# The gated linear attention stage of a decoder layer, its eight groups rewritten

## The reference

```python
q = jax.nn.silu(x @ Wq); v = x @ Wv
log_f = jax.nn.log_sigmoid(x @ Wk + delta); k = -jnp.expm1(log_f)
# per head, over the tokens t:
S = S * jnp.exp(g_t)[..., None] + k_t[..., None] * v_t[..., None, :]
o_t = jnp.einsum('bhk,bhkv->bhv', q_t, S)
# then
o = o * jax.nn.sigmoid(x @ G1 @ G2)
og = og * jax.lax.rsqrt(jnp.mean(og * og, axis=-1, keepdims=True) + EPS)
x = layernorm(x + (og.reshape(B, T, E) * norm_w) @ Wo)
```

## Time and profile before

| | us |
|---|---|
| median of 3 runs | 784.97 (783.91 to 785.06) |
| span of the profiled execution | 781.0 |
| TensorE, VectorE, ScalarE, POOL busy in it | 583.7, 576.7, 404.8, 348.8 |
| first stage, start to the last write of X | 0 to 219.2 |

### The profile page before, as it was taken

One profiled execution on the slowest core, in us unless ns is written; L12 is line 12 of the kernel. 1 busy time (PEld: TensorE's weight loads), 2 busy tenths in 40 slices (PEclk: granted clock), 3 DMA queues, 4 the chain that ended last, 5 costly groups with the idle time before them and its releaser, 6 DMA issues.

```text
span 781.0 us, 18314 instructions
## 1 busy us (share of the span) xinstructions
PE 583.7 (75%) x4172; PEld 468.7 (60%) x4172; DVE 576.7 (74%) x1999; ACT 404.8 (52%) x1107; POOL 348.8 (45%) x445
## 2 busy tenths in 40 slices
PE   4576888778657899999999988239999999993000
PEld 1355666666546677777777756128888888883000
DVE  4888898898535788888988975676666666652998
ACT  1456654556224666666666653027666666663111
POOL 2611111011001137667667775637777777775000
PEclk9687787667656999999999985559999999998555
DMA  5000001000073012122121111243333333333653
GB/s 176 0 15 14 15 13 31 4 0 0 1 215 88 15 35 62 57 60 60 55 60 53 41 49 51 73 99 81 96 97 101 98 101 97 93 100 82 219 193 99
DMA packets 62705, 54.64 MB, mean 70 GB/s; under 512 B 16748, under 2 KB 52146, under 8 KB 62416
## 3 DMA queue, kind: packets, MB, share of 16 engines
q1 hardware_dynamic: 52816, 36.86, 17.1%
q0 software_dynamic: 8704, 16.87, 6.9%
q10 hardware_dynamic: 1152, 0.53, 0.3%
HBM read 29.96 MB, written 21.11 MB: 65 GB/s over the span
## 4 chain that ended last, share of the span: by engine, by line
PE 48%; DVE 19%; DMA 11%; issue 11%; SPq 4%; ACT 3%; POOL 2%; DVEq 1%; POOLq 0%; ACTq 0%
PE bank L781 6%; DMA ys<-yout,xin 5%; PE bank L788 4%; DMA xin<-xs 4%; PE bank L655 4%; PE bank L664 4%; PE bank L629 3%; PE bank L620 3%; DVE r L1450 3%; PE bank L646 3%; PE bank L539 3%; PE bank L773 2%; DVE Rq L1101 2%; DVE mx L1251 2%; PE bank L556 2%
## 5 line engine op out<-in xcount | busy, mean ns | idle before, releaser
L498 POOL DMA_INDIRECT ys<-yout,xin x144 | 145.8, 1013 | 54.4 <-issue 38.2
L479 POOL DMA_INDIRECT xs<-xrow,slots x128 | 130.5, 1019 | 50.7 <-issue 43.5
L996 ACT ACTIVATE hid<-bank,wcur 128x128 f32<-128x128 f32 x292 | 91.4, 364 | 41.1 <-PE bank L781 40.3
L781 PE MATMUL bank<-xinT,wcur 128*128 128x128 f32 x584 | 100.3, 295 | 0.6 <-issue 0.2
L1406 DVE COPY wcur<-wall 128x642 f32 x148 | 74.9, 508 | 20.9 <-DVE gates L1397 0.9
L788 PE MATMUL bank<-wcur,hid 128*128 128x128 f32 x576 | 88.5, 277 | 0.0
L1251 DVE TENSOR_REDUCE mx<-bank 128x4 f16<-128x308 f32 x128 | 60.0, 469 | 33.5 <-PE bank L629 31.9
L781 PEld LDWEIGHTS bank<-xinT,wcur 128*128 128x128 f32 x584 | 77.8, 194 | 8.5 <-issue 3.2
L1413 DVE TENSOR_TENSOR yout<-bank,wcur 128x128 f32<-128x128 f32 x144 | 42.0, 291 | 53.3 <-PE bank L788 51.9
L931 ACT ACTIVATE Ex<-bank 77x512 f32<-77x512 f32 x128 | 75.2, 588 | 5.1 <-PE bank L646 4.4
L788 PEld LDWEIGHTS bank<-wcur,hid 128*128 128x128 f32 x576 | 76.7, 194 | 0.0
(11 more groups left out here) (212 smaller groups left out, 1355.2 us busy)
## 6 DMA issues: line engine op xcount, KB each, us to landing
xin<-xs SPq DMA_DIRECT2D x156, 64.5 KB, 1.8
yin<-ys SPq DMA_DIRECT2D x16, 512.0 KB, 3.7
ys<-yout,xin POOLq DMA_INDIRECT x144, 2.3
xTg<-xT_dram SPq DMA_DIRECT2D x8, 256.0 KB, 2.8
X<-x_dram SPq DMA_DIRECT2D x1, 2048.0 KB, 8.3
x1s<-X SPq DMA_DIRECT2D x32, 64.0 KB
wall<-w_dram SPq DMA_DIRECT2D x1, 2048.0 KB, 8.5
X<-xrow SPq DMA_DIRECT2D x32, 64.0 KB
```

What stands on the lines that cost most here:

```text
L479: pool.indirect_dma_start(words, bass.IndirectOffsetOnAxis(ap=slots[p][:, r:r + 1], axis=0), xrow[p][:, r, 0:RW], None).then_inc(s(f"scatt ...
L498: pool.indirect_dma_start(ys, bass.IndirectOffsetOnAxis(ap=xin[p][:, :].bitcast(U32)[:, E:RW], axis=0), yout[p][:, :], None, bounds_check= ...
L781: mm = pe.matmul(psH[p % 3][:, c * P:(c + 1) * P], wcur[p % QUAD][:, c * P:(c + 1) * P], xinT[p % 4][:, :], start=True, stop=True)
L996: act.activation(hid[p % 3][:, c, :], psH[p % 3][:, c * P:(c + 1) * P], ACT.Gelu, bias=wcur[p % QUAD][:, 2 * I + c:2 * I + c + 1]).then_in ...
```

## The change

The changed stage computes the same sums with other tiles:

- Exponentials are taken of the raw projections in PSUM and capped afterwards; one logarithm and one exponential over 1536 columns serve forgetting, query and gate. The gate weight G1 G2 is multiplied out once.
- Distances to the anchors are formed for the middle token of each block of 8 (64 columns a level in place of 512). Level sides are the leaf sides times such small weights. Key sides, distances and `k` move to POOL; query sides stay on VectorE.
- Levels 64 and 32 are multiplied head by head, 64 rows each, into halves of one bank per head, and copied by ScalarE without a mask. Levels 16 and 8 keep masked copies. Leaves use 64-row tiles and one masked copy of 1024 columns.
- `attended` puts values on the stationary side, so its output is already turned; the head's mean square comes from a matmul with ones.
- Groups are written out, in a new order, and the DMAs of weights are split by first use.

```diff
-            sp.dma_start(xTg[0][:, :], A["xT"][:, 0:GC]).then_inc(s("xT_in0"), 16)
-            for name, t in zip(weights_dma, (wk, wq, wv, wo, g1, g2, delta, norm_w, cwq, cwqT, cwkvT, cwcT, rw, rb)):
+            sp.dma_start(wk[:, :], A["wk"]).then_inc(s("wk_in"), 16)
+            sp.dma_start(xTg[0][:, :], A["xT"][:, 0:GC]).then_inc(s("xT_in0"), 16)
...
@@ POOL, a group
+            def first_part_step(g):
+                keys1(g)             # k = ee * sg, 512 columns
+                leaf_keys(g)         # Kleaf = k * eK, 512; free(A_ps, 4 * g)
+                level_keys(g, 0)     # Lk = Kleaf * wK, 256 columns each
+                level_keys(g, 1).then_inc(s("keys_ready"), 1)
+                level_keys(g, 2).then_inc(s("keys_ready"), 1)
+                level_keys(g, 3).then_inc(s("keys_ready"), 1)
+                if g + 1 < NG:
+                    leaf_decay(g + 1)    # 512 columns
+                    level_decay(g + 1)   # 4 x 64 columns
@@ TensorE
+                for b in range(GB):      # near_levels: level 64, then level 32
                     for h in range(H):
+                        pe.matmul(psN[h][0:64, b * 64:(b + 1) * 64], Lk[0][HP[h], b * T:b * T + 64], Rq[0][HP[h], b * 64:(b + 1) * 64], start=True, stop=True)
+                for n in range(2):
+                    rows = slice(64 * n, 64 * n + 32)
+                    for b in range(GB):
+                        for h in range(H):
+                            mm = pe.matmul(psN[h][rows, 256 + b * 32:256 + (b + 1) * 32], Lk[1][HP[h], b * T + 64 * n:b * T + 64 * n + 32],
+                                           Rq[1][HP[h], b * 64 + 32 * n:b * 64 + 32 * n + 32], start=True, stop=True)
...
+                        mm = pe.matmul(psN[h][:, c], Kleaf[HP[h], c], Qleaf[HP[h], c], start=True, stop=True)   # leaves
...
+                        mm = pe.matmul(psO[HP[h], b * T:(b + 1) * T], v[g % 2][:, b * E + h * DH:b * E + (h + 1) * DH], AT[g % 2][:, h, b, :], start=True, stop=True)   # attended
...
+                pe.matmul(psM[:, :], headsum[:, :], osq[:, :], start=True, stop=True).then_inc(s("ms_ps"), 1)
...
+                    far_level(g - 1, 3)
+                    far_level(g - 1, 2)
+                    leaves(g - 1)
+                    forgets(g + 1)
+                    attended(g - 1)      # waits: taken, v_ready, near_taken
+                    queries1(g + 1)      # two matmuls of 512 columns
+                    head_sums(g - 1)
+                    values1(g + 1)
+                    near_levels(g)       # waits: keys_ready, query_sides, taken
+                    project_out(g - 1)
@@ ScalarE
+                act.activation(ee[:, 1:3, :], ps[:, 1:3, :], ACT.Exp, scale=-1.0).then_inc(s("exps"), 1)
+                act.activation(ll[:, :, :], ee[:, :, :], ACT.Ln, bias=1.0).then_inc(s("logs_ready"), 1)
+                act.activation(sg[g % 2][:, :, :], ll[:, :, :], ACT.Exp, scale=-1.0).then_inc(s("sig_ready"), 1)
...
+                    squares(g - 1)
+                    forget_exp(g + 1)
+                    query_exp(g + 1)
+                    head_scales(g - 1)   # ln and exp, 512 columns each
+                    logs(g + 1)
+                    near_take(g)
+                    sigmoids(g + 1)
+                    value_copy(g + 1)
+                    leaf_exp(g + 1)      # 2 x 512
+                    scales(g - 1)
+                    level_exp(g + 1)     # 2 x 256
+                    normal(g - 1)
@@ VectorE
+                    gated(g - 1)
+                    leaf_queries(g)
+                    level_queries(g, 2).then_inc(s("query_sides"), 1)   # 2 x (64 x 256)
+                    level_queries(g, 0)                                 # 128 x 256
+                    level_queries(g, 1).then_inc(s("query_sides"), 1)   # 128 x 256
+                    cap_forget(g + 1)    # 512 columns
+                    cap_query(g + 1)     # 1024 columns
+                    level_queries(g, 3).then_inc(s("query_sides"), 1)   # 2 x (64 x 256)
+                    head_norm(g - 1)
+                    scan(g + 1)
+                    residual(g - 1)
+                    level_take(g, 3)
+                    moments(g - 1)
+                    level_take(g, 2)
+                    combined(g - 1)
+                    leaf_take(g)         # 1024 columns
+                    shift(g - 1)
+                    query(g + 1)
```

More of the change, by code:

```diff
@@ L395, in _ @@
             setup_steps["masks"] = n
[L397 to L402, removed]
             def leaf_decay(g):
-                pool.wait_ge(s("scan_steps"), 2 * g + 1)
+                pool.wait_ge(s("scanned"), g + 1)
+                free(pool, "decay_exp", 2 * g - 1)
@@ L445, in _ @@
             setup_steps["cross"] = n
-            with pool.Fori(1, NG) as g:
-                key_logs(g)
-                leaf_decay(g)
+            for g in range(3, NG):
+                first_part_step(g)
             words = xs.rearrange("n w -> (n w)").unsqueeze(1)
@@ L503, in _ @@
         def _(pe):
[L504 to L513, removed]
[L514 to L522 removed]
+            psU, psQ, psG, psV = banks[0], banks[1], banks[2], banks[0]
@@ new lines, in _, with forgets, queries1 @@
+            psN, psL = banks[3:5], {2: banks[5], 3: banks[6]}
+            psO, psM, psY, psW = banks[7], banks[7], banks[7], banks[7]
+            HP = [slice(h * DH, (h + 1) * DH) for h in range(H)]
+            def forgets(g):
+                pe.wait_ge(s(f"xT_in{g % 2}"), 16 * (g // 2) + 16)
+                free(pe, "v_ready", g)
+                pe.matmul(psU[:, :], wk[:, :], xTg[g % 2][:, :], start=True, stop=True).then_inc(s("u_ps"), 1)
+            def queries1(g):
+                free(pe, "q_ready", g)
+                pe.matmul(psQ[:, :], wq[:, :], xTg[g % 2][:, :], start=True, stop=True)
+                pe.matmul(psG[:, :], wg[:, :], xTg[g % 2][:, :], start=True, stop=True).then_inc(s("qg_ps"), 1)
@@ L544, in leaves @@
[L544 to L552 removed]
+                pe.wait_ge(s("keys_ready"), 4 * g + 1)
@@ L565, in project_out @@
-            def project_out(g):
-                pe.wait_ge(s("oT_ready"), g + 1)
-                for b in range(GB):
-                    mm = pe.matmul(psY[:, b * E:(b + 1) * E], oT[:, b * T:(b + 1) * T], won[:, :], start=True, stop=True)
-                mm.then_inc(s("y_ps"), 1)
-            pe.wait_ge(s("weights_in"), WN)
-            pe.wait_ge(s("pool_setup"), setup_steps["masks"])
-            pe.wait_ge(s("won_ready"), 1)
-            project_in(0, 0, 16, first=True)
-            gates(0)
@@ L870, in step @@
+            act.wait_ge(s("ndelta_ready"), 1)
+            forget_exp(0)
+            act.wait_ge(s("wg_ps"), 1)
+            act.activation(wg[:, :], psW[:, 0:E], ACT.Copy).then_inc(s("wg_ready"), 1)
+            query_exp(0)
+            logs(0)
+            sigmoids(0)
+            value_copy(0)
+            leaf_exp(0)
+            level_exp(0)
+            act.wait_ge(s("dve_setup"), dve_setup["zeros"])
+            for g in range(NG + 1):
+                if g >= 1:
                     squares(g - 1)
-                if attend:
-                    decay(g, NL)
@@ L1123, in gated @@
[L1123 to L1130 removed]
+            psQ, psL, psO, psY = banks[1], {2: banks[5], 3: banks[6]}, banks[7], banks[7]
```

586 lines of the change are left out of this document (282 added, 304 removed).

## The result

The changed kernel takes 713.73 us (median of 4 runs, 711.67 to 715.5) against 784.5 us (783.91 to 785.06): ratio 0.9098, 95% interval 0.908 to 0.9116. The forecast was 703, its range 692 to 728.

The account below looks back on a forecast made before the run. VectorE bounds the first stage before the change, TensorE's queue after; that stage ends at 22.2 + 7 x 13.5 + 20.3 = 137.0 instead of 219.2 us, so span 698.8, plus 3.97 gives 703 us; range 692 to 728.

Parts of the forecast that it names:

- Start: First stage up to the first near-level matmuls: they begin at 22.2 us, after scan, POOL's distances and keys.
- Period: Time per group in the first stage: 11.3 / 0.90 + 0.9 = 13.5 us, taken seven times.
- TensorE's queue itself ends last: Walk through one group: TensorE's queue sets the period, with 0.5 us for the leaf copy and 0.4 for hand-overs.
- a sign that the walk missed a wait: Listed sign of error: TensorE waiting over 2 us a group for VectorE or ScalarE.
- the shared port sets the period: Rival: POOL's SBUF work blocks VectorE for half of its 7.2 us, 14.9 us a group, 713 us; chance 0.14.
- Tiles: TensorE's half-array matmuls run side by side: leaves and attended 0.97 us each, near levels 2.0 us a group.
- in series: Rival: half-array matmuls run one after the other, or drain; 18.8 us a group, 744 us; chance 0.11.
- Clock: TensorE's granted clock in the first stage, taken as 0.90, between 0.84 and the cross-attention stage's 1.00.
- end: Tail of the first stage, from the last near levels to its end: 20.3 us.
- Engine sums: Work per group after the change: VectorE 11.3 us, ScalarE 11.9, POOL 7.2, TensorE 11.3 at full clock.
- What follows: Stages behind the first: same code, started by the same transfer, so costed at nothing.
- 3.97: Microseconds by which the median of the runs stood above the profiled span, added to the 698.8 us span.

Follow-up runs that it names:

- e2: Changed kernel plus an unneeded 512-column GpSimd product, reading SBUF, behind the keys of seven groups; 0.9311 of the kernel before, unchanged control 0.926.
- e3: Changed kernel plus an unneeded 1400-column GpSimd memset, reading no SBUF, behind the keys of seven groups; 0.9316 of the kernel before, unchanged control 0.926.
- e9: Changed kernel with GpSimd's later-stage constants built early, plus the far level of half blocks of 8 moved ahead of the output projection; 0.9001 of the kernel before.
- e1: Changed kernel with GpSimd's constants for later stages built ahead of group 0 instead of between the first groups; 0.918 of the kernel before, control 0.926.
- e4: Changed kernel with the two heads' half-array matmuls (leaves, attended, level 64) issued one head after the other; 0.9298 of the kernel before, control 0.926.
- e8: Changed kernel with GpSimd's later-stage constants built early, plus redundant TensorE matmuls in the last two rounds; 0.8946 of the kernel before.

## Why the prediction was right, and where it was not

The median lies 10.7 us above the forecast of 703 (10.9 above the 702.8 of the sum) and inside the range. By the prediction's own steps:

- **Start**: 22.2 forecast, 24.18 measured. The scan ended at 16.1 as worked out (16.2); behind it GpSimd's keys and VectorE's query sides held each other up: the four of L437 took 3.03, and the leaf side and the level sides for the near levels took 5.4 us, where the same three lines take 2.4 a group later, with hardly a GpSimd product beside them (33.21 to 35.59). L580 waited for the last of them, 0.34, a path that the prediction does not have. +2.0.
- **Period**: 13.5 forecast; 13.1 in the steady part, a mean of 14.4. +6.6 over seven. The steady size was right for a wrong reason, which is luck. The step that failed is "TensorE's queue itself ends last": it waits over 2 us a group for VectorE, which the last paragraph had named as a sign that the walk missed a wait. The missed one is through GpSimd and the shared port. The rival "the shared port sets the period" had that mechanism and gave 14.9 a group; e2, e3 and e9 show it, at 13.1. That the rival's end (146.8) and time (713) are those measured is chance: in the steady groups its 14.9 was wrong, and the mean of 14.4 came from the early ones. The port stretches VectorE's own instructions by only 0.8 us a group (`nm` 0.50 for 0.16, the leaf side 0.82 for 0.70, the pair 1.18 for 0.84; in all 12.2 busy where 11.3 was forecast); its price lies in the place of GpSimd's 7.8 us in the circle.
- The 9.6 us by which the four early intervals exceed 13.1 were in no step: I costed GpSimd's new work, 7.2 us a group, and not what the unrolled order puts ahead of it. The same constants stood in the kernel before, from 23.8 to 35.9, where GpSimd had 2.3 us to do in a period of 23 and its next product waited 4.3 us for ScalarE. e1 gives 7.9 to 8.7 of the 9.6 back.
- **Tiles**: taken at 0.97 each; leaves 1.09 and attended 1.03 by pitch, near levels 1.2 instead of 2.0. The rival "in series" (744) is refuted, and e4 shows that it was also overpriced: 1.3 us of matmuls a group moved the steady interval by 0.3. By the Trainium skill's rule on drains between tilings (TensorEngine Tiling (Array Packing), Key Properties) the sum would have been nearer 16.3. The trace shows nothing of that size: the leaves' 64*128 tiles start 1.88 us behind the sixteen full-array records ahead of them and the next full-array matmul 1.09 us behind the leaves, with no idle time at either change (102.49, 104.37, 105.46).
- **Clock**: 0.90 forecast, and 0.90 is the mean from 30 to 130 us, but of 1.00 in the steady part, 0.66 behind two of the late keys and 0.50 in stretches of the tail. The last is why the **end** took 21.9 instead of 20.3 (+1.6): the sum had the tail's matmuls at full clock, and e8 prices the error at 3.1 us in all. At full clock the end took 19.1, so the rest of that sum was 1.2 too long.
- **Engine sums**: ScalarE 11.9 forecast, 11.9 by the stretch from 100 to 120 (18.16 x 13.1 / 20); GpSimd 7.2, 7.8, since 256 columns with repeated weights take 0.72 and not 0.62, and the small ones 0.32 and not 0.27.
- **What follows**: costed at nothing, +2.6, and the median stands 2.1 above the profiled span instead of 3.97, -1.8. 2.0 + 6.6 + 1.6 + 2.6 - 1.8 = 11.0. In every run whose time and span are both on record the time stands 1.75 to 2.2 above the span, so the 3.97 held some 2 us of difference between executions, which the prediction took for a constant.

Why the rest grew by 2.6 us wasn't tried; the four executions of the changed kernel differ by 3.8 among themselves. Nor was a version with GpSimd's level keys on another engine, which would cut the circle itself.

## What to carry to other kernels

When work moves to an engine that had time to spare, list everything that its queue already holds between the new steps, for the first groups too: a load of set-up that held nothing up at 10% use cost 8 us at 60%. Look for the circle that closes, engine by engine, before adding up the busiest one: with VectorE 93% busy, "VectorE-bound" and "TensorE-bound" both predicted the wrong price for a microsecond, and the removal of a wait (e9) bought nothing. A queue that runs dry at the end of a stage also slows what comes last in it; cheap filler matmuls bought 3 us.

## What the runs showed of the hardware

- Blocking on the shared port depends on what GpSimd reads: 1.93 us beside a product, 1.18 beside a memset of equal length. It hits even a VectorE instruction of 4 columns: `nm` took 0.50 in the steady groups (0.75 in e9), 0.16 in the tail, where GpSimd is idle, and 0.15 at 63.22, where GpSimd writes memsets.
- Matmuls of two heads that follow each other on different halves of the array ran 1.4 to 1.5 times as fast as those in series (1.71 to 1.16 and 1.55 to 1.09 for sixteen records), not twice.
- Two chips ran the first stage alike (ends 147.23 and 146.46), and what follows it differently: 564 us and 706 us of the span for the same kernel. What in the later stages differs was not pursued.
